# A first mixing on 32-row tiles, placed between two convolutions, with swapping PSUM bank sets

## What is computed

```python
x = x + mix(x, L0)      # out[b] = (sum_k att[b,k] * weight[k]) @ x[b] + att[b] @ bias_k
x = x + conv(x, L1)     # 9 taps, 4 groups, plus c_weight @ cond[b] + side
x = x + mix(x, L2)
x = x + conv(x, L3)
# att[b] = softmax(MLP(cond[b])); everything in fp32
```

## Time and profile before

| | |
|---|---|
| median of 3 runs | 2650.08 us (2649.07 to 2650.8) |
| the profiled execution | 2650.44 us, its span 2648.6 us |
| granted TensorE clock over the span | 0.999 of full |
| PE busy | 2627.4 us (99%) |
| DVE busy | 2143.3 us (81%) |
| ACT busy | 2034.7 us (77%) |
| POOL busy | 818.0 us (31%) |
| DMA queue q1, share of 16 engines | 58.7% |

### The profile page before, as it was taken

One profiled execution on the slowest core, in us unless ns is written; L12 is line 12 of the kernel. 1 busy time (PEld: TensorE's weight loads), 2 busy tenths in 40 slices (PEclk: granted clock), 3 DMA queues, 4 the chain that ended last, 5 costly groups with the idle time before them and its releaser, 6 DMA issues.

```text
span 2648.6 us, 106673 instructions
## 1 busy us (share of the span) xinstructions
PE 2627.4 (99%) x42610; PEld 1808.4 (68%) x42610; DVE 2143.3 (81%) x3093; ACT 2034.7 (77%) x3605; POOL 818.0 (31%) x1040
## 2 busy tenths in 40 slices
PE   9999999999999999999999999999999999999997
PEld 6667666766676667666766676667666766676665
DVE  8888788878887888788878887888788878887884
ACT  7777777777777777777777777777777777777774
POOL 1233233323332333233323332333233323332332
PEclk9999999999999999999999999999999999999999
DMA  4565556555655565556555655565556555655554
GB/s 166 182 205 185 180 184 195 187 180 184 196 187 180 184 195 187 180 183 196 187 180 183 194 189 180 183 195 188 180 183 195 188 180 183 195 189 180 182 176 149
DMA packets 228046, 489.82 MB, mean 185 GB/s; under 512 B 47016, under 2 KB 129072, under 8 KB 195376
## 3 DMA queue, kind: packets, MB, share of 16 engines
q1 hardware_dynamic: 228016, 489.39, 58.7%
HBM read 205.04 MB, written 150.99 MB: 134 GB/s over the span
## 4 chain that ended last, share of the span: by engine, by line
PE 98%; DVE 1%; ACT 0%; issue 0%; DVEq 0%; ACTq 0%
PE ps L361 42%; PE ps L342 28%; PE ps L313 14%; PE ps L326 13%; DVE y L680 0%; DVE y L674 0%; DVE xp L652 0%; DVE m_sum L632 0%; DVE prod L627 0%; PE ps L259 0%; DVE y_full L703 0%; PE ps L428 0%; PE ps L301 0%; PE ps L264 0%; DVE x_t L715 0%
## 5 line engine op out<-in xcount | busy, mean ns | idle before, releaser
L361 PE MATMUL ps<-y,conv_parts 32*128 32x512 f32 x18432 | 1141.7, 395 | 3.9 <-DVE y_full L703 1.8
L361 PEld LDWEIGHTS ps<-y,conv_parts 32*128 32x128 f32 x18432 | 906.5, 183 | 283.1 <-issue 131.4
L781 POOL COPY bias<-bias_table 128x4 f32 (+3 forms) x512 | 317.6, 621 | 1795.5 <-DMA o_ch<-o_ph 896.9
L680 DVE TENSOR_TENSOR y<-y_full,y 128x512 fp32r<-128x512 f32 x1020 | 636.6, 688 | 221.9 <-ACT y L497 221.9
L342 PE MATMUL ps<-y_full,conv_raw 32*32 32x512 f32 (+1 forms) x16384 | 753.8, 596 | 1.7 <-DVE y_full L703 1.7
L491 ACT ACTIVATE y_full<-ps,bias 128x512 f32<-128x512 f32 x1016 | 602.6, 707 | 26.6 <-issue 16.2
L546 ACT ACTIVATE o_ph<-ps,bias 128x512 f32<-128x512 f32 x508 | 308.5, 693 | 371.5 <-PE ps L361 371.5
L497 ACT CAST y<-y_full 128x512 fp32r<-128x512 f32 x1020 | 566.8, 663 | 0.7 <-DVE y_full L703 0.7
L342 PEld LDWEIGHTS ps<-y_full,conv_raw 32*32 32x32 f32 (+1 forms) x16384 | 275.5, 116 | 408.4 <-issue 406.2
L787 POOL COPY o_t<-o_ch 128x512 f32<-128x512 f32 x508 | 528.5, 1186 | 26.9 <-DMA o_ch<-o_ph 26.9
L491 ACT ACTIVATE y<-ps,bias 128x512 fp32r<-128x512 f32 x516 | 313.0, 690 | 191.3 <-PE ps L342 176.6
(11 more groups left out here) (60 smaller groups left out, 74.6 us busy)
## 6 DMA issues: line engine op xcount, KB each, us to landing
x_t<-x SPq DMA_DIRECT2D x128, 1024.0 KB, 5.0
o_ch<-o_ph SPq DMA_DIRECT2D x2032, 64.0 KB, 2.0
out<-o_t SPq DMA_DIRECT2D x127, 1024.0 KB, 4.0
m_parts<-mixed SPq DMA_DIRECT2D x512, 128.0 KB, 2.6
mixed<-m_own SPq DMA_DIRECT2D x128, 128.0 KB, 1.7
conv_raw<-conv_w SPq DMA_DIRECT2D x2, 768.0 KB, 9.8
mix_sb<-mix_w SPq DMA_DIRECT2D x2, 576.0 KB, 7.4
out<-x_t SPq DMA_DIRECT2D x4, 256.0 KB, 4.2
```

Of the source, the lines that this page charges most:

```text
L361: ins = nc.tensor.matmul(ps[:, bank + t, :], conv_parts[layer][rows, w, s - DENSE[0], :], src[rows, a, p_in, q:q + N], start=first, stop=f ...
L680: nc.vector.tensor_tensor(dst, full, high.bitcast(fp32), ALU.subtract).then_inc(low_set[layer], 1)
L781: nc.gpsimd.tensor_copy(bias[layer][:], bias_table[:, bass.ds(j, 1), COLUMN[layer]:COLUMN[layer] + WIDTH[layer]].rearrange("c j g -> c (j ...
```

## The change

PE's order within a step, the banks, and the shape of the first mixing:

- The two bank sets swap roles from step to step (`own_banks`, `other_banks`). Conv 1, the first mixing of sample i+1 and the second mixing of sample i all run in a step's own set; conv 3 of sample i-1 runs in the other.
- The lots of both convolutions with tiles of one shape stand together: `NARROW` of conv 1 and of conv 3, then `WIDE` of conv 1 and of conv 3.
- The first mixing stands between the `WIDE` lots and `dense(3)`, one sample ahead instead of two. From sample 3 (`WHOLE`) on it runs on 32-row tiles, 12 rounds of four; `x` is loaded by four transfers, quarters of time on quarters of the lanes, and its matrix goes through the scratch tensor as that of layer 2 does (one more store, four more loads).
- `free0` waits for `low_1` of the same step (`low_set[1]`), `free1` for the output of sample i-2 (`phases_set`), and `full_2` is awaited ahead of the last shift of `dense(1)` (`third_ready`).
- ACT, DVE, POOL and SP follow in a new order; `y1_full` is one buffer instead of two.

The diff, cut:

```diff
-                sp.dma_start(flat(x_t, "q n"), x[j]).then_inc(x_in, 16)
+                if isinstance(j, int) and j < WHOLE:
+                    sp.dma_start(flat(x_t, "q n"), x[j]).then_inc(x_in, 64)
+                    return
+                for q in range(G):
+                    sp.dma_start(x_t[CG * q:CG * (q + 1)],
+                                 x[j].rearrange("(g c) (q n) -> q c g n", g=G, q=G)[q]).then_inc(x_in, 16)
...
+                if tiled:
+                    store_matrix(0, i + 2)
+                if moves:
+                    shuffle(i - 1, 0)
+                if has(i, inner, -1):
+                    store_matrix(2, i + 1)
+                if moves:
+                    shuffle(i - 1, 1)
+                if tiled:
+                    load_matrix(0, i + 2, False)
+                if moves:
+                    shuffle(i - 1, 2)
+                    shuffle(i - 1, 3, i + 1 if inner else None)
+                if has(i, inner, -1):
+                    load_matrix(2, i + 1, False)
                 if has(i, inner, -3):
                     sp.wait_ge(x_low_set, 4 * (i + 2))
                     load_x(i + 3)
...
+            def first_mix(j, bank, wait_bank):
+
+                pe.wait_ge(m_in[0], 16 * G * (j - WHOLE + 1))
+                pe.wait_ge(x_low_set, 4 * j)
+                for g in range(G):
+                    for n, (m, a) in enumerate(PASSES):
+                        first, final = g == 0 and n == 0, g == G - 1 and n == len(PASSES) - 1
+                        for q in range(G):
+                            rows = slice(CG * q, CG * (q + 1))
+                            if first:
+                                wait_bank(q)
+                            ins = nc.tensor.matmul(ps[:, bank + q, :], m_parts[0][rows, g, m, :], xp[rows, a, g, :], start=first, stop=final)
+                            if final:
+                                ins.then_inc(mm[0], 1)
...
                 def free0(q):
                     if inner or i > 0:
-                        pe.wait_ge(phases_set, nth(i - 1, q))
+                        pe.wait_ge(low_set[1], nth(i, q))
...
-                    dense(1, y1, True, free1)
+                    dense(1, y1, own, free1, third_ready)
...
-                    sparse(1, y1_full[odd], False, free1)
+                    sparse(1, y1_full, own, NARROW)
...
+                if has(i, inner, 1):
+                    sparse(3, y3_full, other, NARROW)
+                if has(i, inner, 0):
+                    sparse(1, y1_full, own, WIDE)
+                if has(i, inner, 1):
+                    sparse(3, y3_full, other, WIDE)
...
+                elif has(i, inner, -1):
+                    first_mix(i + 1, own, free0)
                 if has(i, inner, 1):
-                    if not inner and i == 1:
-                        pe.wait_ge(conv_set, 2)
-                    pe.wait_ge(full_set[2], 4 * i)
-                    sparse(3, y3_full, True, free3)
                     pe.wait_ge(low_set[2], 4 * i)
-                    dense(3, y3, False, free3)
+                    dense(3, y3, other, lambda t: None, lambda: None)
                 if has(i, inner, 0):
-                    second_mix(i)
-                if has(i, inner, -2):
-                    first_mix(i + 2, free0)
+                    second_mix(i, own, free2)
...
+                if has(i, inner, 0):
+                    high_1(i, own_banks(odd), False)
                 if has(i, inner, -1):
-                    full_0(i + 1, 1 - odd)
-                high_2(i - 1, not inner and i == 1)
+                    full_0(i + 1, own_banks(odd))
+                    high_0(i + 1)
+                output(i - 1, other_banks(odd), not inner and is_last(i), not inner and i == 1)
+                if has(i, inner, 0):
+                    full_2(i, own_banks(odd), False)
+                    high_2(i, False)
                 if has(i, inner, -2):
                     x_high(i + 2)
-                if has(i, inner, 0):
-                    high_1(i, False)
-                if has(i, inner, -1):
-                    high_0(i + 1, 1 - odd)
-                output(i - 1, not inner and is_last(i), not inner and i == 1)
-                if has(i, inner, 0):
-                    full_2(i, False)
```

More of the change, by code:

```diff
@@ L28, in build_cond_resid @@
     FIRST = 5 * 128 + 4 + 4 * K
+    WHOLE = 3
     COLUMN, WIDTH = (0, 1, G + 1, G + 2), (1, G, 1, G)
@@ L750, in step @@
                     halves(2, i + 1)
-                    low_0(i + 1, 1 - odd)
-                if not inner and i in (B - 2, B - 1):
-                    full_2(i)
+                if has(i, inner, 0):
+                    if not inner and i == B - 1:
+                        full_2(i, own_banks(odd))
+                    low_2(i)
+                if has(i, inner, -2):
+                    x_low(i + 2)
                 if not inner and is_last(i):
```

222 lines of the change are left out of this document (120 added, 102 removed).

## The result

| | before | changed |
|---|---|---|
| median | 2650.44 us (2649.07 to 2652.06) | 2862.7 us (2858.45 to 2865.75) |
| ratio of the times | | 1.0798 (95%: 1.0785 to 1.0811) |
| span of the profiled execution | 2648.6 us | 2864.0 us |
| granted TensorE clock over the span | 0.999 | 0.997 |
| one step of PE in the loop | 20.38 us | 22.00 us (mean of 117) |

The change makes the kernel 8% slower. The forecast was 2817 us, with 2785 to 2870 around it: the side and the mechanism hold, and the time is 46 us over the forecast.

The account below looks back on a forecast made before the run. PE was taken to bound the kernel. A step was 19.79 of PE's work + 1.84 + 0.07 of waits = 21.70 us; 38.9 + 3.6 + 126 x 21.70 + 39.1 = 2815.8 us of span, 2817 us forecast, range 2785 to 2870.

Parts of the forecast that it names:

- The wait for `low_1`: Ahead of the first mixing, PE waits for DVE's last subtraction on conv 1's banks: 1.84 us in each step.
- S: Start of conv 1's last wide pass in a step; DVE's last subtraction was to end at S + 4.12.
- the fourth matmul: Last of the first mixing's first round over four banks; it can't start before S + 4.17.
- the account: A step is PE's own work plus what the fourth matmul of the first mixing waits for `low_1`.
- PE's own stages: PE's work alone in a step, with fewer changes of shape: 19.79 us, a gain of 0.59.
- narrow pair: Narrow lots of conv 1 and conv 3 together: four passes at 0.43 and one surcharge, 1.93 us.
- second wait: Ahead of dense 1, PE waits for the output's eviction from conv 3's banks: 0.07 us, bounds 0 and 0.3.
- What stays hidden: Other engines' work and transfers that PE should not wait for; first matrix landing about 1.8 us ahead of the first mixing.
- the fast rival: Behind the wide lots: eviction over within S + 2.33, so only changes of shape count; about 2576 us, chance 0.05.
- this ring: First matrix's way from first mixing through casts, halves, store, shuffle and load to the next; forecast gave 1.8 us to spare.
- The ends: Outside the regular steps: 38.9 us before dense 1 of step 1, 3.6 of delay, 39.1 for the last part.
- the third rival: SP's queue or matrix loads come late, so PE waits for the matrix too: 2943 us at 1 us, chance 0.06.

Follow-up runs that it names:

- n3_pool: n3_last with POOL's copies into time order cut to 32 of 512 columns, output left incomplete: 2708.43 us, a single time.
- b_pairs: The kernel before with only the lots paired by shape, narrow of conv 1 and conv 3, then wide of both: 2663.34 us, 1.0058.
- n3_last: The changed kernel with the narrow lot of conv 3 moved behind the wide lots of both convolutions: 2861.87 us, 1.0812 of the kernel before.
- b_tiles: The kernel before with its first mixing as 12 rounds of four 32-row tiles on operands not regrouped, so numbers differ: 2624.91 us, 0.9897.
- split_evict: The changed kernel with conv 1 evicted by ACT and DVE at once, two banks each, first mixing waiting for these copies alone: 2865.2 us, 1.0818.
- whole: The changed kernel with every sample's first mixing on the full array, in its new place, without scratch tensor for its matrix: 2654.01 us, 1.0023.
- split_early: early with the eviction of conv 1 also split between ACT and DVE as in split_evict: 3254.15 us, 1.2281 of the kernel before.
- early: The changed kernel with the first matrix's halves made ahead of low_0, its store and load ahead of all shuffle transfers: 3249.05 us, 1.2259.

## Why the prediction was right in the main and 46 us short

**The wait for `low_1`: right.** This term carries the forecast. From S to the fourth matmul lie 4.17 us forecast, 4.16 in the step shown, 4.21 in the mean of 117 steps. `n3_pool` confirms it from another side, as a single time: its step, 20.78, is the account's 20.76.

**PE's own stages: one term wrong.** The mean step against the forecast, in us:

| part of the step | forecast | measured |
|---|---|---|
| dense 1, its wait included | 4.42 | 4.54 |
| narrow pair | 1.93 | 2.31 |
| wide lots to S | 1.34 | 1.34 |
| S to the fourth matmul | 4.17 | 4.21 |
| fourth matmul to dense 3 | 2.84 | 2.64 |
| dense 3 and second mixing | 7.00 | 6.96 |
| sum | 21.70 | 22.00 |

The mis-sized term is the pair of narrow lots: "That the pair of narrow lots runs at 0.43 a pass isn't shown", and it doesn't run so. It measured 2.31, 0.38 more, while the forecast allowed for 0.05. `b_pairs` shows it without the rest of the change. No row of before has two narrow lots in a row; the nearest bound on record was the 2.14 of two lots apart, and even that is too low. The other miss goes the other way: 2.64 instead of 2.84 behind the fourth matmul. By then three tiles had had a matmul each; in `n3_last`, where none had, the same stretch is 2.86.

The misses add up to 0.54 one way and 0.24 the other, and that they cancel in part is luck. The top of the range, 2870, had its allowance mostly from a second wait of 0.3; what filled it was the pair of narrow lots.

The Trainium skill (TensorEngine Tiling (Array Packing), Key Properties) says that a change of tiling mode drains TensorE, and by that rule fewer changes should gain. Two runs weigh it: `b_tiles` removes two changes of shape and gains 0.23 us a step, which agrees; `b_pairs` removes one between lots and loses 0.09. The rule alone is no guide where the lots that are put together run slower for it.

**The second wait, for the output: inside its bounds, over its 0.07.** Dense 1 with it took 4.54, 0.12 over the forecast's 4.42. The list of waits has its weight loads wait for ACT 110 times, 22.5 us in all, 0.2 each; the forecast's bounds were 0 and 0.3.

```profile
PEld ps L407 <- ACT o_ph L604: 22.5, 110, 0.4
```

**"What stays hidden": right as a schedule, wrong as a reserve.** The matrix came 1.63 us ahead of the fourth matmul, against 1.8 forecast. In that step it let the first one go at S + 2.53 instead of 2.33, which costs nothing while the fourth decides. But the fast rival was priced at 2576 us as if this ring had no end: with the eviction short, the step was to be 19.79. `split_evict` made the eviction short and gave 22.02. The ring takes 20.36 as it stands and 19.87 with POOL's copies cut, and in `n3_last` and `split_evict`, where the wait for `low_1` is gone, it lengthens, because POOL's copies then meet `low_0`. The error did not touch the forecast, since its limit came first, but the rival's time was wrong by 289 us.

**The ends: 10 us short.** Of the 48.2 us between the spans (2864.0 against 2815.8), 126 x 0.30 = 37.8 are the steps; 10.4 are the ends. Dense 1 of step 1 started at 37.91, against 38.9 forecast. From there to dense 1 of step 127, at 2820.85, the steps took 10.9 us more than 126 x 22.00, where the forecast had 3.6; the rest of the span took 43.15 against 39.1, with a wait of 1.93 for the last sample's matrix in it. The loads come late in a few of the first and of the last steps; the dearest wait of each:

```profile
121.76 3.54 PE L359 MATMUL ps<-xp,m_parts 32*128 32x512 f32 x36 [3.00 <-DMA m_parts<-mixed]
...
2810.41 3.05 PE L359 MATMUL ps<-xp,m_parts 32*128 32x512 f32 x48 [3.36 <-DMA m_parts<-mixed]
```

These two steps took 25.12 and 24.06 us. This is the third rival (the matrix late), at the ends only.

**What stays open.** `n3_last` and `split_evict` end at 22.01 and 22.02, as the changed kernel does at 22.00. The links show why each is so long, but not why three kernels should meet there; it may be chance. Why the four `shuffle` issues behind the output take 2.43 us in one kernel and 2.92, 3.07 or 3.78 in others is not settled either: they come sooner after the output's issue there, and no run changed that alone. And no run takes the first matrix's ring out of the changed kernel and leaves all else: `n3_pool` also has the lots in another order, `whole` another form of the first mixing.

## What to carry to other kernels

When an operation goes into banks that another engine has to leave, ask in which order it touches them: one bank after the other rides along behind a staircase of evictions, a round over all of them waits for the last. A slack read from a trace holds for that pace alone; before pricing a shorter step, close the ring of every load (from its consumer back through casts, store, queue and landing), and see which engines will then work at the same time. On a queue that one engine issues in order, transfers between a store and its load are what hides the landing; moving the load up puts that time in front of everything else.

## What the runs showed of the hardware

**A subtraction on DVE slows down beside a copy on POOL.** Both operands in SBUF, 128 x 512: 2.50 us for four alone, 4.00 with POOL copying for 3.04 us of it, and 2.50 again with POOL's copies cut (`n3_last`, `n3_pool`). Over the whole trace of `n3_last` a subtraction of this kind (`low_0` or `low_2`) that POOL's copies cover wholly has a median of 1.38 us (212 of them) and one that they don't touch 0.69 (683). The Trainium skill (SBUF — State Buffer, SBUF: two separate sides) says that a VectorE operation with two SBUF inputs and a GpSimd operation that reads SBUF exclude each other for whole instructions; the trace agrees in kind, and the 1.38 against 0.69 is its price here. The forecast had not weighed this. DVE's subtraction from PSUM was not slowed: in the kernel before 486 of its 516 were covered by POOL's copies, with the same median of 0.74 us as the other 30. The four from 1314.19 took 2.73 us, while POOL copied:

```profile
1313.35 4.13 POOL L787 COPY o_t<-o_ch 128x512 f32<-128x512 f32 x4
```

**A second lot of 16 unsplit 32 x 32 tiles runs worse than the first.** 2.27 to 2.31 us for the two, of which 1.07 are one lot with its change of shape; lots of eight 32 x 64 tiles follow each other at 0.43 a pass. The second lot's loads are spread over 0.56 us where the first's take 0.23; why is not shown.

**The granted clock fell where PE stood for long once a step.** PE waits for the second matrix 124 times in `split_early`, 385.8 us in all or 3.1 each, and its mean clock is 0.922. In `early` it is 123 times, 247.9 us or 2.0 each, and 0.973. In `n3_last` PE waits 117 times for the first matrix, 130.9 us or 1.1 each, with 0.996; in the changed kernel, whose wait is broken up by single matmuls, the mean is 0.997. What decides between them is not isolated. A second mixing of `split_early` in its timeline, and the window of that stretch (busy us and counts by engine; the granted clock is the third number from the end):

```profile
1314.92 4.77 PE L375 MATMUL ps<-y,m_parts 32*128 32x512 f32 x47 [1.81 <-DMA m_parts<-mixed]
```

```profile
1314.92:1319.30 4.38, 4.38 (x50) 4.38 (x54) 4.35 (x4) 0.97 (x2) 4.16 (x6) 0.66 0.95 242
```

Behind a wait of 1.81 us the stretch was run at 0.66 of 2.4 GHz, so in part at the lower level of 1.2 GHz. It cost little here, since the wait for the matrix took it up: `early`, with its higher clock, has the same step within 0.02 us.
